# Sharing out the end of a two-stage kernel: the last group's PSUM banks and order, a row of products for TensorE, and marks in pieces

## What is computed

```python
D = sqrt(max(aa + bb - 2 * ctx @ layernorm(x).T, 0))            # 64 x 512 per batch
R[i, j] = D[i, j] + min(R[i-1, j], R[i, j-1], R[i-1, j-1])      # the cost table
path    = backtrack(R)              # from the last cell to the first, diagonal preferred
x       = x + sum of ctx[i] over the cells (i, j) of the path
h       = relu(quant(layernorm(x) @ w1.T + b1));  x = x + (quant(h) @ w2.T + b2)
```

## Time and profile before

| what | value |
|---|---|
| median of 3 runs | 180.54 us (180.29 to 180.70) |
| the profiled execution | 180.89 us, of which 179.1 us lie between first and last instruction (the span) |
| busy in the span | DVE 152.6 us (85%), PE 109.9 us (61%), ACT 104.8 us (59%), POOL 40.4 us (23%) |
| mean granted TensorE clock | 0.813 of full |
| forward walk, meeting, backward walk on DVE | about 34 to 64.4, 64.4 to 67.9, 67.9 to 96 us |
| network on PE | about 104 to 174.7 us, then the last stores |

### The profile page before, as it was taken

How to read it: one execution, slowest core, us unless ns; L and a number is a source line. 1 busy time by engine, 2 the same in 40 slices (tenths; PEclk the granted TensorE clock), 3 DMA queues, 4 the chain that set the end, 5 groups by cost and what they waited for, 6 DMA issues and landing times.

```text
span 179.1 us, 3484 instructions
## 1 busy us (share of the span) xinstructions
PE 109.9 (61%) x1109; PEld 75.4 (42%) x1109; DVE 152.6 (85%) x737; ACT 104.8 (59%) x195; POOL 40.4 (23%) x101
## 2 busy tenths in 40 slices
PE   6998960000167800000009779999999999989990
PEld 6797950000135400000003335656666666656670
DVE  4999968999999999999999389998898989894341
ACT  3786676799994000044050289877768686868700
POOL 7954895000000000000000000032232222224150
PEclk9999998555555665555555999999999999999997
DMA  5996019300059800020212421007272918284567
GB/s 158 353 352 200 5 16 370 114 0 0 2 185 340 299 0 0 0 75 0 73 50 93 64 37 26 0 0 78 43 83 36 106 20 113 11 109 54 63 69 169
DMA packets 19554, 16.88 MB, mean 94 GB/s; under 512 B 5712, under 2 KB 19152, under 8 KB 19408
## 3 DMA queue, kind: packets, MB, share of 16 engines
q1 hardware_dynamic: 14288, 12.69, 22.1%
q0 software_dynamic: 3808, 3.67, 17.6%
q10 hardware_dynamic: 1440, 0.30, 0.8%
HBM read 7.48 MB, written 9.18 MB: 93 GB/s over the span
## 4 chain that ended last, share of the span: by engine, by line
DVE 43%; PE 30%; DMA 7%; POOL 6%; ACT 3%; issue 3%; SPq 2%; ACTq 2%; DVEq 0%; POOLq 0%
PE y L1362 13%; PE h L1343 8%; DMA X<-in_x_dram 6%; DVE Y L1117 6%; DVE R L887 6%; PE t L1343 4%; DVE A L855 3%; DVE enter L1101 3%; DVE carry L875 3%; DVE M L876 3%; DVE bcarry L1100 3%; POOL lengths L476 3%; PE e L1302 3%; ACTq L319 2%; SPq L333 2%
## 5 line engine op out<-in xcount | busy, mean ns | idle before, releaser
L497 POOL DMA_DIRECT2D out_dram<-E x14 | 17.0, 1217 | 126.7 <-DVE E L1087 126.7
L1362 PE MATMUL y<-w2T,XT 128*128 128x256 bf16 x256 | 37.7, 273 | 0.4 <-DVE XT L1077 0.4
L1362 PEld LDWEIGHTS y<-w2T,XT 128*128 128x128 bf16 x256 | 24.9, 98 | 14.7 <-DVE XT L1077 0.7
L668 ACT ACTIVATE h_int<-h,b_s 128x512 int16<-128x512 f32 x37 | 25.3, 686 | 4.9 <-PE h L1343 4.3
L1379 PE MATMUL h<-w1T 128*128 128x512 bf16 x21 | 7.0, 493 | 32.4 <-DVE enter L1101 32.4
L1343 PE MATMUL h<-M,w1T 128*128 128x512 bf16 x74 | 21.9, 380 | 0.5 <-ACT M L661 0.4
L1282 PE MATMUL t<-ident_bf,w_raw 128*128 128x128 bf16 x32 | 4.6, 311 | 24.9 <-ACT w_raw L602 23.3
L674 ACT ACTIVATE code<-Y,shifts 128x640 bf16<-128x640 bf16 x3 | 2.5, 828 | 29.6 <-DVE enter L1101 29.6
L1077 DVE TENSOR_SCALAR XT<-h_int 128x1024 bf16<-128x1024 int16 x28 | 12.1, 439 | 8.6 <-ACT h_int L668 8.6
L1379 PEld LDWEIGHTS h<-w1T 128*128 128x128 bf16 x21 | 2.3, 122 | 36.6 <-DVE enter L1101 33.2
L668 ACT ACTIVATE h_int<-t,b_s 128x512 int16<-128x512 f32 x19 | 13.0, 686 | 3.3 <-PE t L1343 3.0
(11 more groups left out here) (231 smaller groups left out, 289.0 us busy)
## 6 DMA issues: line engine op xcount, KB each, us to landing
X<-in_x_dram SPq DMA_DIRECT2D x8, 512.0 KB, 9.0
out_dram<-E POOLq DMA_DIRECT2D x14, 256.0 KB, 4.4
w_raw<-in_L_ffn_w_dram SPq DMA_DIRECT2D x2, 1024.0 KB, 5.9
out_dram<-b_s SPq DMA_DIRECT2D x2, 1024.0 KB, 5.9
out_dram<-b_s SPq DMA_DIRECT2D x2, 768.0 KB, 9.5
S<-in_ctx_dram SPq DMA_DIRECT2D x1, 512.0 KB, 3.9
out_dram<-E SPq DMA_DIRECT2D x4, 128.0 KB, 3.0
path_dram<-A SPq DMA_DIRECT2D x3, 160.0 KB, 1.8
```

Source lines behind the costliest of these rows:

```text
L497: nc.gpsimd.dma_start(tiles_out[:, b:b + 2, quad_of(g, 2 * h), :], res[:, g % 2, 2 * h:2 * h + 2, :], accum_op=ALU.add).then_inc(out_store ...
L668: nc.scalar.activation(h_int[:, g % 2, n, :], hidden_banks[i % 3][:, :], ACT.Identity, bias=b1_s[:, n:n + 1], scale=1.0 / W_ONE).then_inc( ...
L1362: mm = nc.tensor.matmul(bank67[t // 2][:, t % 2, :], hq[:, g % 2, n, t * P:t * P + P], w2T[:, n, :], start=(n == 0 and not bias), stop=(n ...
```

## The change

1. `meeting_row` leaves DVE's forward slots, and the diagonals 30 to 36 take its place as fillers. PE makes the sum of the first 7 rows: 7 float32 products of a matrix `lane_of_row[c]` (identity scaled by the row mask, made by 7 new ACT instructions after `order_own`) with `R`, each behind the scan that it reads, ahead of `place_tokens`. DVE adds the eighth row, reading the sum from PSUM, behind a new semaphore (`rows_met`).
2. ACT makes the first 6 of the 9 slots of `NL_more`, DVE the last 3. The meeting loses three of its leftover diagonals, and the backward loop its five.
3. The marks come in three pieces: slots 38 and 39 before the first backward scan, then (3, 7) and (0, 3) of `NL_start` inside the steps of slots 38 and 37, between `enter` and the scan.
4. In the last group each tile has a bank of its own (`results`: `bank67[0]`, `bank23[0]`, `bank67[1]`, `bank23[1]`), the parts come in the order 0, 2, 1, 3, 4, 5, 6, 7, and each tile is finished by an instruction of its own once it is done (`y_done`, 4g + t1).
5. `LATE_TURNS` is new: for g = 5 (as before for g = 0) the transposes of group g+2 come after pair n = 6 instead of n = 5, and ACT copies both halves behind rounding 6 instead of one behind 5 and one behind 6.

```diff
+LATE_TURNS = (0, NG - 3)
+LAST_PARTS = (0, 2, 1, 3, 4, 5, 6, 7)
+EARLY_MORE = SLOTS - 3
+MARKS_AT = {SLOTS - 2: (3, CH - 1), SLOTS - 3: (0, 3)}
...
+        met_rows = bank01[1][:, 0:W + 1]
+        def results(g, t0, t1):
+
+            if g == NG - 1:
+                return (bank67, bank23)[t0 % 2][t0 // 2][:, 0:1, :]
+            return bank67[t0 // 2][:, t0 % 2:t0 % 2 + t1 - t0, :]
...
+            for c in range(CH - 1):
+                nc.scalar.activation(lane_of_row[:, c, :], ident[:, :], ACT.Copy,
+                                     scale=last_row[:, c:c + 1]).then_inc(lanes_marked, 1)
...
+            act.wait_ge(step_done, flags_count(EARLY_MORE - 1))
+            nc.scalar.activation(NL_more[:, 0:EARLY_MORE - HR + 1, :], NL[:, HR - 1:EARLY_MORE, :], ACT.Identity,
+                                 bias=shifts[:, 6:7]).then_inc(more_made, 1)
...
-                        if g and n in (5, 6):
+                        if g not in LATE_TURNS and n in (5, 6):
                             copy_xqT(g + 2, n - 5)
-                        if g == 0 and n == 6:
+                        if g in LATE_TURNS and n == 6:
                             for k in range(KH):
                                 copy_xqT(g + 2, k)
...
-                    if s >= HR:
-                        signal(meeting_row(s - HR))
-                    elif s >= 2:
+                    if s >= 2:
                         signal(diagonal(s - 2))
...
-            chained(meeting_row(CH - 1))
+            v.wait_ge(rows_met, 1)
+            chained(last_meeting_row())
...
-            signal(diagonal(HR - 2))
+            signal(diagonal(SLOTS - 3))
...
-            signal(nc.vector.tensor_scalar(NL_more[:, :, :], NL[:, HR - 1:SLOTS, :], 1.0, None, ALU.add))
+            signal(nc.vector.tensor_scalar(NL_more[:, EARLY_MORE - HR + 1:, :], NL[:, EARLY_MORE:SLOTS, :], 1.0, None, ALU.add))
...
             chained(nc.vector.transpose(bests_T[:, 0, :], bests[:, 0, :]))
-            signal(diagonal(SLOTS - 1))
...
-            signal(diagonal(HR - 1))
+            signal(diagonal(SLOTS - 1))
...
-            signal(diagonal(HR + 6))
+            signal(diagonal(SLOTS - 2))
...
-            signal(diagonal(HR + 5))
+            v.wait_ge(more_made, 1)
...
-                v.wait_ge(y_done, 4 * g + 2 * h + 2)
+                v.wait_ge(y_done, 4 * g + t1)
...
-            start_at(CH, CH + 1).then_inc(back_done, 1)
+            start_at(CH - 1, CH + 1).then_inc(back_done, 1)
...
-                    if HR <= s - 2:
-                        signal(diagonal(s - 2))
...
-                v.wait_ge(back_done, n)
+                entered = n
+                if s in MARKS_AT:
+                    start_at(*MARKS_AT[s]).then_inc(back_done, 1)
+                    n += 1
+                v.wait_ge(back_done, entered)
...
-                if s == SLOTS - 1:
-                    start_at(0, CH).then_inc(back_done, 1)
-                    n += 1
...
-                if g:
+                if 0 < g < NG - 1:
                     finish(g, 0, 2)
...
-                    finish(g, 2, 3)
-                    finish(g, 3, 4)
+                    for t in range(4):
+                        finish(g, t, t + 1)
...
+            pe.wait_ge(lanes_marked, CH - 1)
+            for c in range(CH - 1):
+                pe.wait_ge(step_done, scan_count(HR + c))
+                mm = nc.tensor.matmul(met_rows, lane_of_row[:, c, :], R[:, HR + c, :], start=(c == 0), stop=(c == CH - 2))
+            mm.then_inc(rows_met, 1)
             for g in range(2):
                 place_tokens(g)
...
-                        output(g, n)
+                        output(g, LAST_PARTS[n] if g == NG - 1 else n)
...
-                    if g + 2 < NG and n == (5 if g else 6):
+                    if g + 2 < NG and n == (6 if g in LATE_TURNS else 5):
                         tokens_T(g + 2)
```

More of the change, by code:

```diff
@@ L134, in align_ffn_kernel @@
         meet = sb("meet", [P, W + 1])
+        lane_of_row = sb("lane_of_row", [P, CH - 1, P])
         meet_min = sb("meet_min", [P, W])
@@ L253, in align_ffn_kernel @@
         own_marked = sem("own_marked")
+        lanes_marked = sem("lanes_marked")
+        rows_met = sem("rows_met")
+        more_made = sem("more_made")
         x1_ready = sem("x1_ready")
@@ L326, in load_outer, with scan_count, flags_count @@
             queue.dma_start(PB[at:at + HR, :, W * c:W * c + W], src).then_inc(path_in_outer[j], 16)
+        def scan_count(row):
+            return 5 * row - 6
+        def flags_count(s):
+            return scan_count(s + 3) + 1
         def back_count(lo):
-            return 3 + 4 * (SLOTS - lo)
+            return 4 + 4 * (SLOTS - lo)
         def load_x(queue, k, a):
@@ L862, in signal, with last_meeting_row @@
                 ins.then_inc(step_done, 1)
[L864 to L868, removed]
+            def last_meeting_row():
+                return nc.vector.scalar_tensor_tensor(out=meet[:, :], in0=R[:, SLOTS - 1, :], scalar=last_row[:, CH - 1:CH],
+                                                      in1=met_rows, op0=ALU.mult, op1=ALU.add)
             def forward(lo, hi):
@@ L961, in _ @@
             chained(nc.vector.transpose(bests_T[:, 0, :], bests[:, 0, :]))
-            signal(diagonal(SLOTS - 1))
-            diagonals_at = {SLOTS - 1: steps[0]}
             chain_wait(1)
@@ L971, in _ @@
                                                    in1=bests_T[:, 1, :], op0=ALU.is_equal, op1=ALU.mult))
-            signal(diagonal(HR + 6))
-            diagonals_at[HR + 6] = steps[0]
+            signal(diagonal(SLOTS - 2))
             chain_wait()
             chained(nc.vector.reduce_max(start[:, :], chosen[:, :], mybir.AxisListType.X))
-            signal(diagonal(HR + 5))
-            diagonals_at[HR + 5] = steps[0]
+            v.wait_ge(more_made, 1)
             chain_wait()
@@ L982, in start_at @@
                                                       in1=NL_more[:, lo:hi, :], op0=ALU.not_equal, op1=ALU.mult)
-            v.wait_ge(step_done, diagonals_at[SLOTS - 1])
+            v.wait_ge(step_done, steps[0])
             def steps_of(s):
-                if s in diagonals_at and s < SLOTS - 1:
-                    v.wait_ge(step_done, diagonals_at[s])
                 return nc.vector.scalar_tensor_tensor(out=code[:, s, :], in0=A[:, s, :], scalar=1.0,
@@ L1087, in finish @@
                 nc.vector.scalar_tensor_tensor(
-                    out=res[:, g % 2, t0:t1, :], in0=bank67[h][:, t0 % 2:t0 % 2 + t1 - t0, :],
+                    out=res[:, g % 2, t0:t1, :], in0=results(g, t0, t1),
                     scalar=1.0 / (ACT_ONE * W_ONE), in1=X[:, first:first + 2 * (t1 - t0) - 1:2, :],
@@ L1107, in _ @@
                         on_path(s + 1, PIECE_AT[p - 1])
-                    if HR <= s - 2:
-                        signal(diagonal(s - 2))
-                        diagonals_at[s - 2] = steps[0]
-                v.wait_ge(back_done, n)
+                entered = n
[3 more added lines that the diff above has]
+                v.wait_ge(back_done, entered)
                 if s >= HR - 1:
@@ L1359, in output @@
                 if bias and n0 == 0:
-                    nc.tensor.matmul(bank67[t // 2][:, t % 2, :], ones[:, :], b2_rows[:, :], start=True, stop=False)
+                    nc.tensor.matmul(results(g, t, t + 1)[:, 0, :], ones[:, :], b2_rows[:, :], start=True, stop=False)
                 for n in range(n0, n0 + NH // 2):
-                    mm = nc.tensor.matmul(bank67[t // 2][:, t % 2, :], hq[:, g % 2, n, t * P:t * P + P], w2T[:, n, :],
+                    mm = nc.tensor.matmul(results(g, t, t + 1)[:, 0, :], hq[:, g % 2, n, t * P:t * P + P], w2T[:, n, :],
                                           start=(n == 0 and not bias), stop=(n == NH - 1))
```

## The result

The changed kernel takes **178.93 us**, the median of 4 runs (178.72 to 179.23), against 180.62 for the kernel before on the same chip (4 runs, 180.29 to 180.99): a ratio of 0.9907, 95% interval 0.9882 to 0.9932. A second measurement of the same file gave 0.9928 (0.9906 to 0.9951). On 180.54 us that is 1.7 and 1.3 us less, where the prediction had 1.14. The profiled execution took 178.78 us with a span of 177.0.

What follows compares the result with a forecast made beforehand. DVE's chain bounds the walks and meeting, then PE sets the pace, then stores through full DMA engines. Terms -0.41 + 0.05 + 0.01 - 0.12 - 0.17 - 0.30 - 0.20 = -1.14 off 180.54 give 179.4 us, range 178.3 to 180.0.

Steps and rivals of the forecast that it cites:

- Forward: DVE's forward walk: a diagonal in place of a meeting row shortens seven slots from 0.784 to 0.726 us, -0.41.
- Row sum by PE: Last meeting row waits for PE's seventh product: 0.77 against 0.755 us, +0.05; row 0.03 to 0.1 after scan 38.
- (b): Rival, chance 0.11: PE's row sum is late by its upper bound, +0.60 instead of +0.05, giving 179.95 us.
- (d): Rival, chance 0.05: PE's products can't keep step with the scans, the seventh 3.6 us late, giving about 182.9 us.
- The PSUM read: DVE's last meeting row reads the sum from PSUM instead of SBUF, +0.01 us.
- The meeting: DVE's meeting: shorter NL_more and a dropped filler gain, a larger first mark costs 0.07; together -0.12 us.
- Backward: DVE's first two backward steps: marks in pieces replace diagonals, 1.04 and 0.98 for 1.40 and 0.72 us; -0.17.
- The turn: PE around group 5: pair 6 before the transposes removes a wait, product 0 of group 7 comes sooner, -0.30 us.
- Rival (c): Chance 0.09: PE's wait around group 5 only moves, tokens to product 0 stays as long, giving 179.7 us.
- The last group: End of the kernel: last store issued up to 1.28 us sooner, but full DMA engines leave only -0.20.
- Rival (a): Chance 0.18: SP's chain of store issues, not the DMA engines' load, sets the end; 1.28 us counts, giving 178.3.

Runs made afterwards that it cites:

- padded kernel of before: Nine small float32 products more on PE behind place_tokens, against the kernel before: 180.17 us, ratio 0.9988; without POOL's transfers of group 6: 179.33 us, ratio 0.9916.

## Why the prediction was right, and where not

The direction and the size of the whole came out: -1.14 forecast, -1.3 and -1.7 measured. Most gains lie where they were forecast. But the terms as the traces show them add up to -0.98 (-0.58 on DVE, -0.40 at the turn, 0.0 for the last group), so that the sum comes so near is in part luck. The terms one by one:

- **Forward**, -0.41: 0.40 in the trace. Right.
- **Row sum by PE**, +0.05: +0.10 (0.48 instead of 0.38 from scan to row). A product takes 0.69, not 0.65. The row starts 0.13 behind the end of scan 38, where 0.03 to 0.1 were to be seen: it does wait, a little. The clock was 0.50, as assumed. Rivals (b) and (d) fell: a wait of 0.22 for each scan shows that no product delays the next.
- **The PSUM read**, +0.01: the row takes 0.28 us, as its predecessor did from SBUF (0.29). The Trainium skill's larger fixed cost for a PSUM source ("VectorE: DVE Perf Modes", section on the TRN2 errata) doesn't show in the length of this row; what lies ahead of its start is not told apart from the wait for the product.
- **The meeting**, -0.12: only -0.04. The three sizes of the sum came out: up to `least` 0.20 was gained (2.13 instead of 2.33 us from the last row), 0.10 by the shorter NL_more and 0.10 by the filler between the transposes, and the larger mark cost 0.07 (0.27 instead of 0.20 to `code`). The step that failed is that the rest of the meeting was put at nothing. It grew by 0.09: from `start` to the mark 0.28 instead of 0.23, although the diagonal between them is gone, from `least` to `start` 0.52 instead of 0.49, where both diagonals still stand, and 0.01 behind `code`. Why is open. (Of the five leftover diagonals of the meeting three are left: it loses two, and not three as the change says.)
- **Backward**, -0.17: -0.21 in the two steps (1.91 instead of 2.12) and another 0.01 a step behind them. Right, within its bounds. From the start of a piece (68.26, 69.25) to its scan are 0.40 and 0.33 us, near the 0.42 and 0.355 of the estimate; the diagonal that each replaced was worth 0.13 or 0.14 (69.20 to 69.34), not 0.10.
- On **DVE** together the trace shows -0.58 at the sixth scan back; forecast -0.64. The run of that part alone gave -0.78 (-1.07 to -0.49). The earlier fetch comes with it, measured by itself as -0.2 (-0.5 to +0.1); that the two make up the 0.78 is arithmetic, not shown.
- **The turn**, -0.30: -0.40 in the trace, just over the bound of -0.37; -0.27 alone (-0.56 to +0.04). The transposes came the 0.15 earlier that was allowed for a late modelled end, and needed 1.78 to product 0 where 1.81 was forecast. Rival (c) fell.
- **The last group**, -0.20, near the end at 0: alone it is 0.0, in two pairs of kernels. That the full engines swallow it was the right reason, and the kernels without group 6's transfers show it: take the accumulations away, and 0.57 comes out. Rival (a), 178.3 by early issues alone, fell. What the prediction took for it, the last issue of before at 176.03, was read as issues behind one another; one of them was 1.1 us longer than the rest beside the fetch. That in the pair of traces above the span ends as much sooner as the issues do is then no proof of (a): the fetch comes late in the one and early in the other. In the whole change 0.3 to 0.7 more than the sum of parts was measured, not resolved against the intervals; whether the last group gives something once the rest is faster stays open.

What was missing is the fetch: a gain of a few tenths (0.2 to 0.4) that belongs to no edit's purpose, and that makes up for the terms that came out smaller. With it the terms give 1.2 to 1.4 us; the rest, up to the 1.7 of the first measurement, is not accounted for.

## What to carry to other kernels

Where the DMA engines are full at the end, finishing only the last tiles sooner bought nothing; first make the transfers cheaper, here by turning the last accumulations into plain stores (1.1 to 1.5 us on top of the change for two bias products). In a chain of short dependent instructions a filler costs only by how much it is longer than the wait that it fills: taking one away gave 0.10 us between the two transposes, 0.01 a step in the backward walk, and nothing ahead of the mark. Read the price off the distances around each place. And a difference of a few tenths of a microsecond may come from the length of a program: vary that alone before an edit gets the credit.

## What was not expected of the hardware

The instruction fetch: 16 KB of the instruction queue took 0.9 to 2.3 us. Where they fell among the last transfers, one DMA engine ended 0.8 to 1.3 us behind the others, and an issue of SP's that met them took 1.1 to 2.7 us instead of some 0.4.

The clip of 1024 int16 elements takes 0.43 us, but 0.6 while POOL issues a transfer. The row of after above (169.63, 0.60) lies within this issue:

```profile
169.22 1.20 POOL L520 DMA_DIRECT2D out_dram<-E  x1 [3.95 <-DVE E L1108]
```

Without POOL's transfers of group 6 the same clip in the padded kernel of before is:

```profile
170.43 0.43 DVE L1077 TENSOR_SCALAR XT<-h_int 128x1024 bf16<-128x1024 int16 x1 [0.71 <-ACT h_int L668]
```

PE's stand behind it is then 0.26 instead of 0.43. The Trainium skill ("SBUF — State Buffer", section on who interferes with whom) has GpSimd share a pair of ports with VectorE's two-port modes, one of them waiting for the other; a slower clip beside POOL's issue fits that, though no run here tells this cause apart from another one. By the same section of the Trainium skill the one that waits is blocked for the other's whole instruction; here the clip ends at 170.23 and POOL's row only at 170.42. In the kernel with half of group 6 plain the clip under POOL's issue took 0.48.
